# Router logits of the second stage: router columns held, tokens moving, small transposes back

## The reference, cut to what matters

```python
x = x + 0.5 * ffn(layernorm(x))        # first stage
x = x + attn(layernorm(x))             # 16 heads, 4 key/value heads, causal
x = x + 0.5 * ffn(layernorm(x))        # second stage, the same weights

def ffn(x):                            # x: 4 x 512 tokens of 256
    scores = x @ router_w              # router_w 256 x 16: logits of 16 experts
    weights, idx = top_k(softmax(scores), 2)
    weights = weights / weights.sum()
    # y = sum over the two experts e of weights * down_w[e](silu(gate_w[e] x) * up_w[e] x)
```

## Time and profile before

| | |
|---|---|
| median of 3 runs | 918.38 us (917.87 to 919.81) |
| the profiled execution | 918.7 us, span 916.9 us, mean granted clock 0.975 |
| busy in the span | PE 810.7 us (88%), DVE 634.3 (69%), ACT 567.1 (62%), POOL 468.3 (51%) |
| pool 2's logits | between 665 and 718 us of the span |
| pool 3's logits | between 803 and 811 us of the span |

### The profile page before, as it was taken

The page is one execution under the profiler, slowest core; times in us unless marked ns, Lnnn a source line. Parts: engine busy times, 40 slices in busy tenths (PEclk is TensorE's granted clock), DMA queues, the critical chain, the costliest instruction groups (busy, mean ns, idle before and its releaser), DMA issues.

```text
span 916.9 us, 16344 instructions
## 1 busy us (share of the span) xinstructions
PE 810.7 (88%) x4904; PEld 687.1 (75%) x4904; DVE 634.3 (69%) x1503; ACT 567.1 (62%) x1458; POOL 468.3 (51%) x409
## 2 busy tenths in 40 slices
PE   4578989879999999998999999998999979799990
PEld 3567868668787888887888887787788767687870
DVE  6525565447887778878777878787766788455573
ACT  3245646557776777767777777676867646355550
POOL 1355413496775845755456555455454537203274
PEclk9999989999999999999999999999999999899995
DMA  9988963220011100000000000000000035456684
GB/s 340 324 277 297 267 170 116 83 39 13 12 15 16 19 1 7 12 7 1 1 1 2 1 2 1 1 3 1 8 1 1 1 149 168 123 151 196 195 241 169
DMA packets 55540, 78.60 MB, mean 86 GB/s; under 512 B 7840, under 2 KB 44320, under 8 KB 54816
## 3 DMA queue, kind: packets, MB, share of 16 engines
q1 hardware_dynamic: 43360, 55.50, 19.0%
q0 software_dynamic: 9216, 16.82, 7.4%
q10 hardware_dynamic: 2880, 5.24, 1.9%
HBM read 42.61 MB, written 34.93 MB: 85 GB/s over the span
## 4 chain that ended last, share of the span: by engine, by line
PE 55%; POOL 14%; issue 11%; DVE 7%; DMA 5%; SPq 4%; ACT 3%; POOLq 0%; ACTq 0%; DVEq 0%
PE ps L1492 46%; PE ps L1681 5%; SPq L705 3%; POOL sb_x L1430 3%; POOL xs L1405 2%; POOL xs L1412 2%; POOL sb_ropeB L1439 2%; POOL sb_xf L1442 2%; PE ps L1549 2%; DMA xs<-sb_wA_raw 1%; POOL sb_wF L1449 1%; DMA xs<-sb_wF_raw,sb_pos 1%; PE ps L1561 1%; DVE sb_nmax L1282 1%; DVE sb_x L1308 1%
## 5 line engine op out<-in xcount | busy, mean ns | idle before, releaser
L1492 PE MATMUL ps<-sb_wF 128*128 128x512 f32 (+3 forms) x1248 | 301.8, 368 | 7.5 <-DVE sb_wF L1299 4.4
L1492 PEld LDWEIGHTS ps<-sb_wF 128*128 128x128 f32 x1248 | 199.3, 192 | 23.3 <-DVE sb_wF L1288 3.3
L1439 POOL TENSOR_TENSOR sb_ropeB<-sb_ropeB,sb_sin 128x512 f32<-128x512 f32 x80 | 107.0, 1337 | 151.9 <-ACT sb_ropeB L885 151.8
L902 ACT ACTIVATE sb_prob<-ps,sb_nmax 128x128 f32<-128x128 f32 (+3 forms) x256 | 134.2, 526 | 62.8 <-DVE sb_nmax L1282 61.7
L1492 PE MATMUL ps<-sb_wF,sb_wA 128*128 128x512 f32 x576 | 156.8, 408 | 7.4 <-ACT sb_ropeB L885 7.1
L1282 DVE TENSOR_REDUCE sb_nmax<-ps 128x1 f32<-128x128 f32 (+3 forms) x256 | 121.9, 485 | 59.1 <-PE ps L1492 57.6
L1449 POOL TENSOR_TENSOR sb_wF<-sb_xf,sb_wF 128x512 fp32r<-128x512 f32 x75 | 98.6, 1315 | 95.3 <-ACT sb_wF L894 95.0
L1308 DVE SCALAR_TENSOR_TENSOR sb_x<-ps,sb_rinv,sb_x 128x256 f32<-128x256 f32 x256 | 122.8, 480 | 23.3 <-PE ps L1492 14.4
L1288 DVE TENSOR_TENSOR sb_wF<-ps,sb_wF 128x512 fp32r<-128x512 f32 x160 | 109.4, 684 | 28.3 <-ACT sb_wF L910 27.6
L1492 PE MATMUL ps<-sb_wA,sb_wF 128*128 128x256 f32 x768 | 115.7, 287 | 10.3 <-DVE sb_x L1308 8.6
L1492 PEld LDWEIGHTS ps<-sb_wF,sb_wA 128*128 128x128 f32 x576 | 103.7, 192 | 27.4 <-ACT sb_ropeB L885 8.2
(11 more groups left out here) (175 smaller groups left out, 1233.1 us busy)
## 6 DMA issues: line engine op xcount, KB each, us to landing
ys<-sb_wA_raw SPq DMA_DIRECT2D x124, 128.0 KB, 2.5
sb_wF_raw<-xs SPq DMA_DIRECT2D x44, 128.5 KB, 3.7
sb_wA_raw<-xs SPq DMA_DIRECT2D x44, 128.5 KB, 2.6
xs<-sb_wA_raw SPq DMA_DIRECT2D x19, 256.0 KB, 12.4
sb_work<-xs SPq DMA_DIRECT2D x36, 128.5 KB, 3.4
sb_wA_raw<-in_wattn ACTq DMA_DIRECT2D x18, 256.0 KB, 4.6
sb_wF_raw<-in_wgu SPq DMA_DIRECT2D x4, 768.0 KB, 15.7
sb_wF_raw<-in_wdn SPq DMA_DIRECT2D x4, 768.0 KB, 22.2
```

The lines of the kernel that those rows point to most:

```text
L902: nc.scalar.activation(prob[k % 2][:, h, 0:(i + 1) * P], ps[:, bank_of((k * G + h) % (UB * G)), 0:(i + 1) * P], ACT.Exp, bias=nmax[:, k % ...
L1439: nc.gpsimd.tensor_tensor(ropeB[:, slot], ropeB[:, slot], sin[:], ALU.mult).then_inc(rope_mul, 1)
L1492: return nc.tensor.matmul(out, lhsT, rhs, start=start, stop=stop)
```

## The change

For pools 2 and 3 `logits` loads the router's 16 columns and moves 256 tokens: two matmuls instead of four, with a result of experts by tokens, 16x256. ACT copies it to SBUF (`turned`), over the first columns of `lx`. PE turns it back with two transposes of 16x128 (`logits_back`), to the same place and shape as before. `lx` is now filled feature slice by feature slice (`lx_part`), so that 256 tokens lie side by side. The next T waits for the copy of the turned-back logits.

```diff
+    def turned_at(q, h):
+        if q.p == 2:
+            return ps[0:E, third_bank(h), 0:2 * P]
+        return ps[0:E, LOGBANKS[q.p], 2 * P:4 * P]
+    def turned_copy(q, h):
+        return lx(q, h)[0:E, 0:2 * P]
+    def copied(q, h):
+        return h + 1 if q.p == 2 else pools[2].nh + h + 1
...
-        "pe": {1: {"T,-1,3": 0, "V,-1,2": 1, "T,0,0": 2, "S,2,0": 3, "T,1,0": 4, "W,-1,1": 5, "T,1,1": 6, "W,0,0": 7},
-               2: {"T,-1,3": 8, "V,-1,2": 9, "T,0,0": 10, "S,2,0": 11}, 3: {"S,0,2": 12}},
+        "pe": {1: {"T,-1,3": 0, "V,-1,2": 1, "W,-2,1": 2, "T,0,0": 3, "S,1,3": 4, "J,0,1": 5,
+                   "T,1,0": 6, "S,2,2": 7, "J,0,2": 8, "T,1,1": 9, "W,0,0": 10, "J,0,3": 11},
+               2: {"T,-1,3": 12, "V,-1,2": 13, "W,-2,1": 14, "T,0,0": 15, "S,1,3": 16, "J,0,1": 17}, 3: {"S,0,2": 18}},
-        "act": {1: {"pt_hi,-1,3": 8, "pt_hi,0,0": 9, "pt_hi,1,0": 10, "pt_hi,1,1": 11},
-                2: {"pt_hi,-1,3": 16, "pt_hi,0,0": 17}, 3: {"exp,0,0": 18}},
-        "dve": {1: {"max,1,1": 14, "max,2,0": 15, "x_add2,-1,1": 16, "x_add2,0,0": 17},
-                2: {"max,1,1": 28, "max,2,0": 29}},
+        "act": {1: {"pt_hi,-1,3": 8, "exp,1,1": 19, "pt_hi,0,0": 9, "rope_hi,0,0": 20, "pt_hi,1,0": 10, "a_hi,0,0": 21,
+                    "pt_hi,1,1": 11, "exp,2,3": 22},
+                2: {"pt_hi,-1,3": 16, "exp,1,1": 23, "pt_hi,0,0": 17, "rope_hi,0,0": 24}, 3: {"exp,0,0": 18}},
+        "dve": {1: {"x_add2,-2,1": 14, "x_add2,-1,0": 15, "Jd,0,2": 16, "Jd,0,3": 17},
+                2: {"x_add2,-2,1": 28, "x_add2,-1,0": 29}},
...
+        def turned(q, h):
+            act.wait_ge(turned_done, copied(q, h))
+            nc.scalar.activation(turned_copy(q, h), turned_at(q, h), ACT.Copy).then_inc(tcopy_done, 1)
...   # ACT, expert steps of pool 2: lx_copy at 7 and 8, turned at 9 and 11, gap_exp at 18 (was 17)
...   # DVE, last_pool: lcopy and route from step 12 (was 10), shares and places at 20 to 23 (were 18 to 21)
@@ logits
+            if q.p >= 2:
+                if q.p == 3 and h > 0:
+                    pe.wait_ge(tcopy_done, copied(q, h) - 1)
+                for k in range(K):
+                    ins = mm(turned_at(q, h), router_w(q, k), lx(q, h)[:, k * 2 * P:(k + 1) * 2 * P], k == 0, k == K - 1)
+                ins.then_inc(turned_done, 1)
+                return
...
+        def logits_back(q, h):
+            pe.wait_ge(tcopy_done, copied(q, h))
+            for t in range(2):
+                ins = nc.tensor.transpose(logits_at(q, h)[:, t * E:(t + 1) * E], turned_copy(q, h)[:, t * P:(t + 1) * P],
+                                          ident[0:E, 0:E])
+            ins.then_inc(logit_done, 1)
             if q.p == 2:
                 projections["logits"] = copies(q, h)
...
-            elif q.p == 2 and i in (8, 9):
-                logits(pools[3], i - 8)
-            elif q.p == 2 and i == 17:
+            elif q.p == 2 and i in (8, 9, 10, 11):
+                (logits, logits_back)[i % 2](pools[3], (i - 8) // 2)
+            elif q.p == 2 and i == 19:
                 ranks(pools[3])
```

More of the change, by code:

```diff
@@ L180, in program @@
     lx_done = sem("lx_done")
+    turned_done = sem("turned_done")
+    tcopy_done = sem("tcopy_done")
     logit_done = sem("logit_done")
@@ L480, in lx_bank, with lx_part @@
         return LXBANKS[(q.halves + h) % 2] if q.n == 0 else third_bank(h) if q.p == 2 else JBANK
+    def turned_at(q, h):
[6 more added lines that the diff above has]
+        return h + 1 if q.p == 2 else pools[2].nh + h + 1
+    def lx_part(q, t, k):
+        at = (t * K + k if q.p < 2 else k * 2 + t) * P
+        return slice(at, at + P)
     def logits_at(q, h, halves=1):
@@ L851, in experts @@
                     first_head(i)
-                elif q.p == 2 and i in (7, 8):
-                    lx_copy(pools[3], i - 7)
-                elif q.p == 2 and i == 17:
+                elif q.p == 2 and i in (7, 8, 9, 11):
+                    (lx_copy if i < 9 else turned)(pools[3], (i - 7) % 2 if i < 9 else (i - 9) // 2)
+                elif q.p == 2 and i == 18:
                     gap_exp(pools[3])
@@ L940, in do @@
                     lx_copy(pools[2], n - 12)
+                elif n == 18:
+                    gap_exp(pools[2])
                 else:
-                    gap_exp(pools[2])
+                    turned(pools[2], n - 19)
         for h in range(pools[0].nh):
@@ L1183, in last_pool @@
                 rows(q, 2 * (i - 4), 2 * (i - 3))
-            elif i == 10:
+            elif i == 12:
                 lcopy(q, 0)
                 route(q, 0)
-            elif 11 <= i < 17:
-                route(q, i - 10)
-            elif i == 18:
+            elif 13 <= i < 19:
+                route(q, i - 12)
+            elif i == 20:
                 shares(q)
                 places(q, 0)
-            elif 19 <= i < 22:
-                places(q, i - 18)
+            elif 21 <= i < 24:
+                places(q, i - 20)
         def experts(n):
@@ L1512, in logit_transposes @@
                 for k in range(K):
-                    ins = nc.tensor.transpose(ps[:, lx_bank(q, h), (t * K + k) * P:(t * K + k + 1) * P],
+                    ins = nc.tensor.transpose(ps[:, lx_bank(q, h), lx_part(q, t, k)],
                                               row(q, 2 * h + t)[:, k * P:(k + 1) * P], ident[:])
@@ L1521, in logits @@
             pe.wait_ge(lx_done, at + 1)
+            if q.p >= 2:
[5 more added lines that the diff above has]
+                return
             for t in range(2):
                 for k in range(K):
-                    ins = mm(logits_at(q, h)[:, t * E:(t + 1) * E], lx(q, h)[:, (t * K + k) * P:(t * K + k + 1) * P],
-                             router_w(q, k), k == 0, k == K - 1)
+                    ins = mm(logits_at(q, h)[:, t * E:(t + 1) * E], lx(q, h)[:, lx_part(q, t, k)], router_w(q, k),
+                             k == 0, k == K - 1)
+            ins.then_inc(logit_done, 1)
[4 more added lines that the diff above has]
+                                          ident[0:E, 0:E])
             ins.then_inc(logit_done, 1)
@@ L1726, in do @@
                     task(b, k, n)
-                elif n == 12:
+                elif n == 18:
                     ranks(pools[2])
-                elif n % 2 == 0:
-                    logit_transposes(pools[2], n // 2)
                 else:
-                    logits(pools[2], n // 2)
+                    (logit_transposes, logits, logits_back)[n % 3](pools[2], n // 3)
         pe.wait_ge(ident_in, 16)
```

1 line of the change is left out of this document (removed).

## The result

| | before | after |
|---|---|---|
| median of 5 runs each, same chip | 919.19 us (917.87 to 919.91) | 927.01 us (925.99 to 929.60) |
| profiled execution, its span | 918.7 us, 916.9 us | 926.4 us, 924.6 us |
| mean granted clock | 0.975 | 0.970 |

The ratio is 1.0091, 95% interval [1.0072, 1.0110]: the change costs 7.8 us. Forecast were 5.6. The 927.0 us lie 0.4 above the end of the stated range (926.6); the median of the kernel before, now of five runs, is 0.8 above the 918.38 from which the range was counted.

What follows compares the result with a forecast made beforehand. PE was taken to bound the kernel (busy 88% of the span). Attention 3.9, pool 3's halves 2.35 and the exponential -0.2 made 6.0 us, less 0.4 swallowed 5.6: forecast 924.0 us (0.63), range 920.4 to 926.6.

Steps and rivals of the forecast that it cites:

- half 1's shape: Pool 2's second half of logits in the attention: same shape as the first, 0.87 us plus 0.15 for ACT's copy.
- the 0.4 that should be swallowed: Taken off the 6.0 us sum, since PE's idle times behind 725 us should swallow some of the delay.
- half 0 costs 0.27 of work and about 0.6 of waiting: Pool 2's first half in the attention: PE's added work and T's wait for DVE's copy behind x_add2,-2,1, 0.87 us.
- Half 2, net 0: Attention: T comes 0.6 us later behind Jd,0,2, but some 0.65 of DVE's blocked norm step goes; -0.5 to +0.7.
- half 3, 0.1: Attention: covered, as the chain behind J,0,3 runs over DVE, ACT and pt_hi, not T,2,0; 0.1 us, up to 0.6.
- first rival: The attention's delays are swallowed and only pool 3's stalls are paid: 920.5 us, chance 0.13.
- Pool 3's halves, 2.35: Expert steps: 0.91 us PE wait for ACT's copy plus 0.2 transposes per half, and 0.14 logits; range 1.5 to 2.8.
- The exponential, -0.2: Expert phase: moved from step 17 to 18 at the same cost, `shares` two steps behind it; -0.5 to 0 us.
- Pool 3's placing, 0: Two steps, 3.0 us, later but hidden by 3.8 us of slack, a scatter landing 1.6 us after its issue ends.
- third rival: Pool 3's placing shows: if `places` and the load's landing slip, PE waits up to 3 us: 927 us, chance 0.09.
- fourth rival: Not slower: DVE's pool 2 routing gets out of POOL's rope time, saving 4.2 us: 919.8 us, chance 0.08.
- second rival: Held columns are cheap, 0.12 us per 256-column pass, saving 0.40 in each of eight halves: 920.8 us, chance 0.07.

Runs made afterwards that it cites:

- e3: Kernel before with only DVE's copies of pool 2's logits moved to the changed kernel's places; 982.51 us, ratio 1.0034 to before.
- e4: Changed kernel with DVE's logit copy ahead of the two x_adds in halves 0, 1, 4, 5; 986.96 us against 980.92 before, ratio 1.0063.
- e9: Changed kernel plus unused PE transposes, 21 around group 3's last W and 15 at expert step 20; 990.63 us, ratio 1.0111 to before.
- e8: Kernel before with half 2's copy behind pt_lo,1,0, pool 3's `shares` one step and `places` two later; 980.43 us against 982.02, ratio 0.9990.
- e7: Changed kernel with pool 3's transposes back one step later, DVE's copy at step 13 with two routing parts; 988.92 us, ratio 1.0061 to before.
- e11: Kernel before, unchanged, run for its trace on another chip; 983.49 us, ratio 1.0018.
- e10: Kernel before with half 2's copy behind pt_lo,1,0, pool 3's `shares` and `places` later, 21 unused transposes around group 3's last W; 982.44 us, ratio 1.0012.
- e1: Changed kernel with pool 3's logits, steps and placing as before, only pool 2 changed; 983.68 us against 980.92 before, ratio 1.0032.
- e5: Changed kernel run again, same code, on another chip; 990.33 us against 982.02 before, ratio 1.0076.
- e2: Changed kernel with pool 2's logits and order lists as before, only pool 3 changed; 982.69 us, ratio 1.0031 to before.
- e6: Changed kernel plus unused PE transposes, 21 around group 3's last W and 15 at expert step 18; 992.94 us, ratio 1.0113 to before.

## Why the prediction was wrong

The direction, both places of cost and the main wait of each were right. What failed is the size of PE's own work, half 1's shape, the 0.4 that should be swallowed, and a term that was not in the sum, the clock.

1. *"So half 0 costs 0.27 of work and about 0.6 of waiting".* The wait held: DVE behind the x_adds, PE answering 0.1 later, 0.80 with no work beside it (e3). The work was mis-sized: 0.69 (e4), not 0.27. Of this the logits are 0.28, not 0.07. Four passes of 256 columns cost 0.24 each, not 0.22, and the first starts 0.20 behind the transpose ahead of it in place of 0.11. This term was priced by counting passes and left out the switch into them. The transposes back are 0.22 by themselves, as forecast, but W ahead and V behind each take 0.1 more, so 0.41. In half 0 of the changed kernel these 0.41 fall inside the wait: from W to T it has 2.20 us (669.66 to 671.86), where the forecast had 2.24 (669.96 to 672.2), so its miss of 0.2 is that of the logits alone.
2. *"Half 1 has the same shape"* was wrong. Half 0's transposes back lie between W and V, in the time that T waits for DVE anyway. Half 1's lie ahead of W, so DVE's chain starts later by them: 1.41 in place of 1.07. The 0.15 allowed for ACT's copy did not come: PE goes on without idle time at 676.97. Halves 4 and 5 repeat 0 and 1. Steps 1 and 2 together are 1.2 of the 1.3 us that the attention was off.
3. *Half 2, net 0, and half 3, 0.1.* Measured -0.07 and 0.25. That the blocked norm step gives time back was right; it gave 1.04 of its 1.20, where the text had 0.65.
4. *"I take 0.4 off, since PE's idle times behind 725 should swallow some".* Nothing was swallowed: 5.18 to 5.20 is the lag at each T from 725 to 748, up to the low clock. The idle time was waiting for DVE and ACT, whose start the same delay moved. The text had this argument against its own first rival and did not use it for the sum.
5. *Not in the sum: the clock.* +1.0 and +1.2 from two stretches of half clock (e9). The first stands where the trace before had 1.00 and no edit is near. The waits of PE ahead of it do not tell the two apart: over the 22 us ahead they are 0.90, 0.43, 1.18, 0.45 and 1.68 us, to 0.03 us, in the kernel before, e3 and e4, which stay at 1.00, and in the changed kernel and e8, which fall to 0.50. What differs there is only when they come. This is the larger failure, and no row of before would have given it; but the profile did show PE waits of 1.3 to 1.9 us close to both places, and the chance of a stretch should have widened the range upwards.
6. *Pool 3's halves, 2.35.* Measured 2.8: waits of 0.79 in place of 0.91, logits 0.25 in place of 0.07. *The exponential, -0.2*: what the later `shares` gave is hidden under the second low clock. Over steps 17 to 25 the lag falls by 0.3 in e7 and 0.4 in e8, which move them and have no low clock there, and by 0.3 in e11, which doesn't move them: 0 to 0.1 is theirs.
7. *Pool 3's placing, 0.* The time was right: the placing moved, SP waited, PE did not. The working was not: the scatter took 3.9 us to SP's load and not 1.6, and what saved the 0 was the 4.1 us between load and use, of which 2.1 are left. The third rival, priced at 927, came out with the right time and the wrong cause.
8. The fourth rival (DVE's comparisons get free of POOL) did not come: 1.25 at 730.80 and 1.47 at 738.48, the same as in the earlier trace rows.

The overshoot was given back in part: -1.9 from step 22 on and -0.6 ahead of the landmark. That the total missed by 2.2 us and not by more is luck. Of the 1.9, 0.4 is not the change's (e11); the rest is open. No experiment on the other chips tells it, since stalls lie among these steps there.

The second rival took W's 0.12 per pass for held columns. The spacing of 0.24 settles it against that price, for float32.

The Trainium skill ("TensorE: Matmul & The Clock Gate", "Back-to-back issue gap") would give some 109 ns for such a pass, an estimate from its formula, if a pass of the trace is one of its matmuls; the trace disagrees, with 0.24 us, and decides. The same page ("HAM oscillation — how this bites in real kernels") describes idle gaps between bursts of matmuls after which the next burst runs at half clock. The trace agrees in that: W's passes take 1.62 in place of 0.95 us behind PE's waits (e8), and with PE filled 0.95 (e10). But the kernel before has the same waits of 1.68 and 0.41 us ahead of W and runs it in 0.95.

## What to carry to other kernels

Before swapping the loaded and the moved operand, price the work that turns the result back by its neighbours too, and look where it falls: inside a wait that exists anyway it is free, ahead of the instruction that feeds the wait it is paid twice. Idle time of an engine swallows a delay only if what ends this idle time is not itself behind the delay. A schedule with many waits of one to two us on TensorE can lose its clock by an edit elsewhere: look at the granted clock by stretch of both traces before explaining a difference by instructions.

## What the runs showed that was not expected

- Two transposes of 16x128 in float32 cost 0.22 us themselves and 0.19 us on the rows around them (W 0.80 for 0.71, V 0.80 for 0.70).
- ACT's copy of 16 partitions by 256 columns takes 0.36 us, that of 128 partitions 0.38 (the earlier trace rows and the changed kernel's L827).
- The granted clock falls at places that an edit far ahead decides, reproducibly: the last units of the attention ran at 0.50 in five of the traces here (after, e1, e5, e7, e8), and in e2 at 0.60 some us earlier (763 to 766), where the lag grew by no more than 0.04; in before, e3, e4 and e11 at 1.00. What decides between them is open, since the waits ahead are the same in both kinds. Work in PE's idle time went with a clock of 1.00 in each of the three kernels that had it at the first place (e6, e9, e10). At the second place one kernel shows it (e9), and there the low clock is absent in e7 too, which has no such work.
- The length of one wait doesn't tell the clock behind it: at the exponential 2.06 us (after) and 2.09 (e5) were followed by 0.50, but 2.03 (e8) and 1.87 by 1.00.
